# Causal mask of transposed attention scores: added by VectorE in PSUM instead of by TensorE, and score pairs taken one by one

## The chip, the cores and the metric

The kernel runs on one core of one Trainium2 chip. The metric is the device time of one execution in microseconds (us). Times of before are the median of three executions. All rows shown come from one further, profiled execution.

## What is computed

A block of a model: a linear-attention layer, a feed-forward layer, a causal softmax attention with two query sets, and the feed-forward layer again, over 2 batches of 1024 rows of 512. The change lies in the causal attention:

```
q = concatenate([q1, q2], axis=1)            # 16 heads of 32 for each set
scores = einsum('bhqd,bhkd->bhqk', q, k2) / sqrt(d)
scores = where(tril(ones((T, T))), scores, finfo.min)
p = softmax(scores, axis=-1)
y = einsum('bhqk,bhkd->bhqd', p, v2)
y1, y2 = y[:, :H], y[:, H:]
y = y1 - sigmoid(x @ Wlam) * y2
return y @ Wo
```

## The kernel before

The attention is a loop over 16 units. A unit is one batch, a group of four heads (HPT) and one of the two query sets. Its order on every engine is written out by hand, and engines meet only at semaphores.

A unit has 12 steps. Step s stands for a block of 512 queries (c = 0 in steps 0 to 3, c = 1 in steps 4 to 11) and a tile of 128 keys, kt. Scores are computed transposed, keys on the partitions and queries along the row. A step is diagonal when its key tile lies inside its query block: steps 0 to 3 and 8 to 11, eight of twelve, 128 of 192 in all. In a diagonal step the query columns before the tile are left out, so the width falls 512, 384, 256, 128.

For a step TensorE issues, in this order:

- `scores` (L1259): four score matmuls in fp32, one for each head with 32 rows of the array (L1265); four matmuls that add minus the row maximum (L1271); in a diagonal step four matmuls of an identity with `later_key`, a 128x128 matrix with -3e38 where the key lies behind the query (L1278). The first pair of heads is released to ScalarE by the second such matmul, the other pair by the fourth.
- `weigh` (L1283) of the step before: probabilities times values, four matmuls, each behind a wait for the exponential of its pair (L1295).
- `row` (L1228) for the next unit, two steps ahead: the scores once more, not transposed, four matmuls (L1237), with their own mask (L1243) in eight of the twelve. VectorE reduces them to row maxima (L1582).
- parts of jobs that fill the time (projections for the next heads L1151, values L1189, sums of the exponentials L1197, the transposed maxima L1201), and in some steps a pair of output matmuls (L1255), which VectorE adds to `x` (L1639).

ScalarE takes the exponentials of a step in two instructions, a pair of heads each (L1441), and copies jobs out of PSUM. GpSimd adds the exponentials up (L1519). VectorE does, within a step, at step 10 the negated maxima (L1592), then the two reductions of the row, the splitting of the transposed maxima into bf16 parts (step 10: L1603, L1605, L1603, L1605, L1610), the output add, and two reciprocals after steps 3, 4, 6 and 7 (L1629).

PSUM has eight banks. Six form a ring of three pairs. `PAIR_USES` lists who takes a pair and when: score pair 0, score pair 1, row pair 0, row pair 1 in each step, and an output pair in some. `take_pair` (L1215) waits until the use three places earlier has been read:

```python
kind, u, s, a = PAIR_USES[n - 3]
if kind == "row":
    pe.wait_ge(row_max, (u * NR + s) * 2 + a + 1)
elif kind == "out":
    pe.wait_ge(out_added, OUTS.index((u, s)) + 1)
else:
    pe.wait_ge(exped, (u * NS + s) * 2 + a + 1)
```

Both `scores` and `row` take their two pairs ahead of the first of four matmuls.

Of the kernel before, what the change touches and what calls it, by code (L numbers as in the profile page):

```python
# [9 lines left out]
ALU = mybir.AluOpType  # L10
# [4 lines left out]
P = 128  # L15
# [5 lines left out]
TPB = BLK // P  # L21
# [825 lines left out]
QT = S // P  # L847
HPT = P // HD
# [5 lines left out]
STEPS = [(c, kt) for c in range(CQ) for kt in range(TPB * (c + 1))]  # L854
NS = len(STEPS)
# [10 lines left out]
def step_width(s):  # L866
    c, kt = STEPS[s]
    return max(kt * P - c * BLK, 0)
# [63 lines left out]
def row_in(u, i):  # L932

    n = u * NS + i + LEAD
    return divmod(n, NR) if n < UNITS * NR else None
# [20 lines left out]
def summed_by(u, s):  # L956

    return sum(1 for t in range(NS) if STEPS[t][1]) * u + sum(1 for t in range(s + 1) if STEPS[t][1])
# [18 lines left out]
def phase_rest(nc, core, wq1, wq2, wk, wv, wlam, wo, out):  # L977
    with ExitStack() as ctx:
        sem = lambda n: ctx.enter_context(nc.semaphore("b_" + n))
# [29 lines left out]
        ident_b, later_key, mask = sb("ident_b", P, BF16), sb("later_key", P, BF16), sb("mask", P)  # L1009
# [11 lines left out]
        scored, exped, weighed, summed = sem("scored"), sem("exped"), sem("weighed"), sem("summed")  # L1021
        y_copied, y_ready, inverted, taken = sem("y_copied"), sem("y_ready"), sem("inverted"), sem("taken")
        out_done, out_added = sem("out_done"), sem("out_added")
        turn_ready, high_kept = sem("turn_ready"), sem("high_kept")
        early_var, early_root = sem("early_var"), sem("early_root")
        e_stats, e_mv = sb("e_stats", CQ * TPB * 6), sb("e_mv", CQ * TPB * 2)
# [28 lines left out]
        def strip(tile, j, lo, hi):  # L1055
            return tile[j * HD:(j + 1) * HD, lo:hi]
# [4 lines left out]
        def pair_banks(use):  # L1061
            at = PAIR_NTH[use] % 3 * 2
            return core["psum"][:, at * BLK:(at + 2) * BLK].rearrange("p (j q) -> p j q", j=2)

        def held(u, s):

            c, kt = STEPS[s]
            if kt == 0:
                return heads(total[(u * CQ + c) % 2])
            return heads(prob[(summed_by(u, s) - 1) % 2])  # L1070
# [68 lines left out]
        def _(pe):  # L1139
# [75 lines left out]
            def take_pair(use):  # L1215

                n = PAIR_NTH[use]
                if n >= 3:
# [7 lines that stand above are left out]
                return pair_banks(use)  # L1226

            def row(u, n):  # L1228
                qt, kc = ROWS[n]
                r, w = divmod(u, 2)  # L1230
                if n == 0:
                    pe.wait_ge(fill_copied, FREED_BY_ACT[NTH[("q", r, w, CQ - 1)]])
                hi = min((kc + 1) * BLK, (qt + 1) * P)
                width, diagonal = hi - kc * BLK, kc == qt // TPB
                to = [take_pair(("row", u, n, a)) for a in range(2)]
                for j in range(HPT):
                    last = pe.matmul(to[j // 2][:, j % 2, 0:width], strip(qT[w][r % 2], j, qt * P, (qt + 1) * P),  # L1237
                                     strip(kT[w][r % 2], j, kc * BLK, hi), start=True, stop=not diagonal)
                    if j % 2 and not diagonal:
                        last.then_inc(row_done, 1)  # L1240
                if diagonal:
                    for j in range(HPT):
                        last = pe.matmul(to[j // 2][:, j % 2, width - P:width], later_key[:, :], ident_b[:, :],  # L1243
                                         start=False, stop=True)
                        if j % 2:
                            last.then_inc(row_done, 1)
# [12 lines left out]
            def scores(u, s):  # L1259
                c, kt = STEPS[s]  # L1260
                r, w = divmod(u, 2)
                off, diagonal = step_width(s), kt >= TPB * c
                to = [take_pair(("score", u, s, a)) for a in range(2)]
                for j in range(HPT):
                    pe.matmul(to[j // 2][:, j % 2, off:BLK], strip(kT[w][r % 2], j, kt * P, (kt + 1) * P),  # L1265
                              strip(qT[w][r % 2], j, c * BLK + off, (c + 1) * BLK), start=True, stop=False)
                if kt == 0:
                    pe.wait_ge(bias_ready, u * CQ + c + 1)
                for j in range(HPT):
                    rows = slice(j * HD, (j + 1) * HD)  # L1270
                    last = pe.matmul(to[j // 2][:, j % 2, off:BLK], ones_b[rows, :],  # L1271
                                     bias[u % 2][rows, c * BLK + off:(c + 1) * BLK],
                                     start=False, stop=not diagonal)
                    if j % 2 and not diagonal:
                        last.then_inc(scored, 1)
                if diagonal:
                    for j in range(HPT):
                        last = pe.matmul(to[j // 2][:, j % 2, off:off + P], ident_b[:, :], later_key[:, :],  # L1278
                                         start=False, stop=True)
                        if j % 2:  # L1280
                            last.then_inc(scored, 1)

            def weigh(u, s):  # L1283
                c, kt = STEPS[s]
# [95 lines left out]
        def _(act):  # L1380
# [48 lines left out]
            def exps(u, s):  # L1429
                c, kt = STEPS[s]  # L1430
                off, g = step_width(s), u * NS + s
                if kt == 0:
                    if u:
                        act.wait_ge(filled, NTH[("den", u - 1, c)] + 1)
                elif summed_by(u, s) > 2:

                    act.wait_ge(summed, summed_by(u, s) - 2)
                    act.wait_ge(weighed, g - 1)
                for a in range(2):
                    act.wait_ge(scored, 2 * g + a + 1)  # L1440
                    act.activation(held(u, s)[:, 2 * a:2 * a + 2, off:BLK], pair_banks(("score", u, s, a))[:, :, off:BLK],  # L1441
                                   ACT.Exp, scale=SCALE).then_inc(exped, 1)

# [112 lines left out]
        def _(dve):  # L1556
# [20 lines left out]
            def row(u, n):  # L1577
                qt, kc = ROWS[n]
                width = min(BLK, (qt + 1) * P - kc * BLK)
                for a in range(2):  # L1580
                    dve.wait_ge(row_done, (u * NR + n) * 2 + a + 1)
                    dve.tensor_reduce(  # L1582
                        maxima[u % 2][:, :].rearrange("p (h q c) -> p h q c", h=HPT, q=QT)[:, 2 * a:2 * a + 2, qt, kc],
                        pair_banks(("row", u, n, a))[:, :, 0:width], AX.X, ALU.max).then_inc(row_max, 1)

            def negate(u):
                dve.wait_ge(row_max, (u + 1) * 2 * NR)
                if u:
                    dve.wait_ge(filled, NTH[("neg", u - 1)] + 1)
                part_of = neg2[:, :].rearrange("p (h n q) -> p n h q", h=HPT, n=4)  # L1590
                for n in range(3):
                    v.did(dve.tensor_reduce(part_of[:, n], maxima[u % 2][:, :].rearrange(  # L1592
                        "p (h q c) -> p h q c", h=HPT, q=QT), AX.X, ALU.max, negate=True))
                v.settle()
                dve.sem_inc(neg_ready, 1)
# [96 lines left out]
                row(*divmod(n, NR))  # L1692
            for u in range(UNITS):
                for i in range(NS):
                    if u == UNITS - 2 and (i + 1, 0) in NORM_AT:
                        early_turn(0, NORM_AT[i + 1, 0])
                    if i == NS - 2 and u + 1 < UNITS:
                        negate(u + 1)
                    if row_in(u, i):
                        row(*row_in(u, i))  # L1700
                    for place in range(2):
                        if (u, i, place) in ENDING and ON_DVE[NTH[ENDING[u, i, place]]]:
                            finish(ENDING[u, i, place])
                    if out_in(u, i):
                        add_out(*out_in(u, i))
                    if i in INVERT_AT:
                        c, half = INVERT_AT[i]
                        if u >= c:
                            invert(u - c, c, half)
                    if u == UNITS - 3 and i < QT // 2:  # L1710
                        early_stats(i)
# [118 lines left out]
```

## Time and profile before

| | |
|---|---|
| median of 3 runs | 2175.33 us (2172.42 to 2177.26) |
| profiled execution, its own time | 2175.0 us |
| its span, first to last instruction | 2172.1 us |
| TensorE busy | 2029.3 us, 93% |
| VectorE busy | 1269.5 us, 58% |
| ScalarE busy | 855.2 us, 39% |
| GpSimd busy | 888.1 us, 41% |
| attention | from about 781 us to 1800 us of the span |

PE is TensorE, PEld its weight loads, DVE VectorE, ACT ScalarE, POOL GpSimd. An fp32 matmul leaves two records, so four heads leave eight. Matmuls overlap: the row of a group gives the time from the first start to the last end, and the next group starts a little before that. A wait is shown in brackets behind the instruction that waited, with the engine and line that ended it.

### The profile page before, as it was taken

What the parts mean: (1) busy time and instruction counts of PE and PEld (TensorE: products, weight loads), DVE (VectorE), ACT (ScalarE), POOL (GpSimd) and SP (SyncE); (2) the same over time, 40 slices, a digit from 0 to 9 for tenths busy, and PEclk for the clock granted to TensorE, in tenths of its full rate; (3) what the DMA queues carried; (4) which work ended last, traced back from release to release, by engine and by line L of the source; (5) the groups of instructions that cost most, each with busy time, mean ns of one, the idle gap of its engine ahead of it and who ended that gap; (6) DMA issues with size and microseconds to landing.
All of it is one profiled execution on the core that took longest, in us unless ns stands there. A gap on an engine that the chain in (4) does not pass through costs nothing.

```text
span 2172.1 us, 29720 instructions
## 1 busy us (share of the span) xinstructions
PE 2029.3 (93%) x11783; PEld 881.1 (41%) x11824; DVE 1269.5 (58%) x1838; ACT 855.2 (39%) x1304; POOL 888.1 (41%) x457
## 2 busy tenths in 40 slices
PE   7999999999999998999999999999998878989999
PEld 3444444444444443343433333333433323444444
DVE  5878778557764643555555555555556633676635
ACT  4534344244444223333343434344343442443431
POOL 3757586400000002676665565766656682000000
PEclk9999999999999998999999999999999998999999
DMA  7101001300000030000000010000000021000001
GB/s 228 38 29 35 29 31 37 133 1 1 1 1 1 1 71 1 4 13 16 16 11 20 11 21 1 16 16 16 1 11 6 13 76 40 1 1 20 20 1 39
DMA packets 69000, 55.55 MB, mean 26 GB/s; under 512 B 36800, under 2 KB 55232, under 8 KB 68608
## 3 DMA queue, kind: packets, MB, share of 16 engines
q1 hardware_dynamic: 61952, 41.07, 6.5%
q10 hardware_dynamic: 6912, 12.59, 1.8%
q8 instruction: 95, 1.56, 0.3%
q14 instruction: 41, 0.34, 0.0%
HBM read 43.02 MB, written 10.62 MB: 25 GB/s over the span
## 4 chain that ended last, share of the span: by engine, by line
PE 50%; ACT 5%; DVE 5%; POOL 3%; issue 2%; ACTq 0%; DVEq 0%; POOLq 0%
PE psum L116 9%; PE psum L1151 8%; PE psum L1237 8%; PE psum L1265 7%; PE psum L140 5%; PE psum L1295 3%; ACT b_probs L1441 3%; PE psum L1189 3%; DVE b_maxima L1582 2%; POOL b_totals L1519 2%; PE psum L1243 2%; PE psum L1278 2%; PE psum L1255 2%; PE psum L1271 1%; PE psum L1197 1%
## 5 line engine op out<-in xcount | busy, mean ns | idle before, releaser
L1519 POOL TENSOR_TENSOR b_totals<-b_totals,b_probs 128x2048 f32<-128x2048 f32 (+3 forms) x160 | 515.2, 3220 | 350.0 <-ACT b_probs L1441 340.5
L1582 DVE TENSOR_REDUCE b_maxima<-psum 128x2 f32<-128x1024 f32 (+3 forms) x384 | 349.9, 954 | 433.1 <-PE psum L1243 249.5
L1441 ACT ACTIVATE b_probs<-psum 128x1024 f32<-128x1024 f32 (+3 forms) x320 | 228.3, 765 | 284.5 <-PE psum L1278 187.6
L435 PE MATMUL psum<-hT,a_win 128*128 128x512 f32 x640 | 290.8, 597 | 2.6 <-DVE a_parts L727 1.2
L116 PE MATMUL psum<-hT,b_early 128*128 128x512 f16 x1024 | 229.0, 383 | 5.2 <-DVE b_middle L202 5.2
L116 PE MATMUL psum<-hT,W 128*128 128x512 f16 x1024 | 229.3, 384 | 3.9 <-DVE a_win L202 3.9
L435 PEld LDWEIGHTS psum<-hT,a_win 128*128 128x128 f32 x640 | 119.4, 191 | 129.3 <-issue 128.0
L116 PEld LDWEIGHTS psum<-hT,b_early 128*128 128x128 bf16 x1024 | 100.7, 99 | 132.5 <-issue 12.1
L116 PEld LDWEIGHTS psum<-hT,W 128*128 128x128 bf16 x1024 | 101.1, 99 | 127.9 <-issue 9.4
L1496 POOL MEMSET b_mask<- 128x128 f32 x1 | 0.2, 205 | 358.8 <-POOLq L267 358.8
L1629 DVE RECIPROCAL b_down<-b_down 128x128 f32<-128x128 f32 x128 | 111.9, 917 | 43.7 <-ACT b_down L1419 43.7
L654 POOL TENSOR_TENSOR a_parts<-a_parts 128x512 bf16<-128x512 bf16 x48 | 60.1, 1252 | 132.8 <-DVE a_parts L730 132.8
L1265 PE MATMUL psum<-b_middle 32*128 32x512 f32 (+3 forms) x768 | 90.9, 542 | 22.7 <-DVE b_maxima L1582 13.2
L1237 PE MATMUL psum<-b_early 32*128 32x512 f32 (+3 forms) x768 | 90.2, 537 | 21.8 <-ACT b_probs L1441 15.1
L1441 ACT ACTIVATE b_totals<-psum 128x1024 f32<-128x1024 f32 x64 | 62.0, 1021 | 123.3 <-PE psum L1278 64.8
L1237 PE MATMUL psum<-b_middle 32*128 32x512 f32 (+3 forms) x768 | 89.1, 530 | 16.9 <-ACT b_probs L1441 14.6
L1265 PE MATMUL psum<-b_early 32*128 32x512 f32 (+3 forms) x768 | 89.4, 534 | 15.3 <-DVE b_maxima L1582 14.4
L202 DVE SCALAR_TENSOR_TENSOR a_win<-psum,a_win 128x512 f32<-128x512 f32 x64 | 44.1, 691 | 101.3 <-ACT a_win L156 100.3
L202 DVE SCALAR_TENSOR_TENSOR b_middle<-psum,lent 128x512 f32<-128x512 f32 x64 | 44.2, 691 | 96.1 <-ACT lent L156 95.5
L1151 PE MATMUL psum<-hT,b_middle 128*128 128x512 f32 x192 | 99.1, 625 | 0.0
L140 PE MATMUL psum<-W,a_yo 128*128 128x512 bf16 x256 | 97.0, 379 | 0.6
L140 PE MATMUL psum<-b_down,b_probs 128*128 128x512 bf16 x256 | 97.0, 379 | 0.6
(225 smaller groups left out, 3181.9 us busy)
## 6 DMA issues: line engine op xcount, KB each, us to landing
a_parts<-in_w_guT ACTq DMA_DIRECT2D x32, 256.0 KB, 2.8
ternary<-W SPq DMA_DIRECT2D x1, 6144.0 KB, 18.3
a_win<-in_w_inT SPq DMA_DIRECT2D x20, 256.0 KB, 7.3
a_parts<-in_w_pT ACTq DMA_DIRECT2D x16, 256.0 KB, 2.6
b_down<-lam_rows SPq DMA_DIRECT2D x32, 128.0 KB, 2.7
b_early<-ternary SPq DMA_DIRECT2D x8, 512.0 KB, 8.3
out<-x SPq DMA_DIRECT2D x16, 256.0 KB, 2.2
x<-in_x SPq DMA_DIRECT2D x3, 1024.0 KB, 8.0
```

The costliest lines, as they stand in the source:

```text
L116: last = pe.matmul(self.bank[m % 2 * 2 + part], self.gu[:, k * 2 * HID + col:k * 2 * HID + col + P], self.hT[:, at:at + BLK], start=(k + h ...
L140: last = pe.matmul(self.down_bank(j, t), src[:, m * BLK + t * P:m * BLK + (t + 1) * P], self.wd[:, m * D:(m + 1) * D], start=(m + half == ...
L202: dve.scalar_tensor_tensor(self.h[:, m * BLK:(m + 1) * BLK], self.bank[m % 2 * 2 + 1], 1.0 / UP, self.sg[m % 2], ALU.mult, ALU.mult).then_ ...
L435: last = pe.matmul(ring(s, j), win[:, at:at + P], core["hT"][:, (i * KT + k) * BLK:(i * KT + k + 1) * BLK], start=(k == 0), stop=(k == KT ...
L1151: return pe.matmul(to, weights[:, k * P:(k + 1) * P], hT[:, at:at + BLK], start=(k == 0), stop=(k == KT - 1))
L1189: last = pe.matmul(to[:, t % 2 * 2 * P:(t % 2 + 1) * 2 * P], hT[:, at:at + P], wv_all[:, k * D + h * P:k * D + (h + 2) * P], start=(k == 0 ...
L1237: last = pe.matmul(to[j // 2][:, j % 2, 0:width], strip(qT[w][r % 2], j, qt * P, (qt + 1) * P), strip(kT[w][r % 2], j, kc * BLK, hi), star ...
L1265: pe.matmul(to[j // 2][:, j % 2, off:BLK], strip(kT[w][r % 2], j, kt * P, (kt + 1) * P), strip(qT[w][r % 2], j, c * BLK + off, (c + 1) * B ...
L1441: act.activation(held(u, s)[:, 2 * a:2 * a + 2, off:BLK], pair_banks(("score", u, s, a))[:, :, off:BLK], ACT.Exp, scale=SCALE).then_inc(ex ...
L1519: pool.tensor_tensor(acc, acc, held(u, s)[:, :, off:BLK], ALU.add).then_inc(summed, 1)
L1582: dve.tensor_reduce(maxima[u % 2][:, :].rearrange("p (h q c) -> p h q c", h=HPT, q=QT)[:, 2 * a:2 * a + 2, qt, kc], pair_banks(("row", u, ...
L1629: last = dve.reciprocal(rden[k % 2][:, cols], rden[k % 2][:, cols])
```

## The change

`scores` no longer issues the third group of four matmuls in diagonal steps. The second matmul of each pair of heads in L1271 releases it. VectorE gets `cap`, which waits for a pair and adds `mask` (fp32, the same -3e38 pattern) to the 128 diagonal columns of both heads, in place in PSUM. ScalarE waits in diagonal steps for `capped` instead of `scored`. `cap` of a step stands first in VectorE's work of that step. In `scores` and in `row` the second pair is taken behind the first pair's two matmuls.

```diff
-                to = [take_pair(("row", u, n, a)) for a in range(2)]
+                to = []
                 for j in range(HPT):
+                    if j % 2 == 0:
+                        to.append(take_pair(("row", u, n, j // 2)))
...
-                off, diagonal = step_width(s), kt >= TPB * c
-                to = [take_pair(("score", u, s, a)) for a in range(2)]
+                off = step_width(s)
+                to = []
                 for j in range(HPT):
+                    if j % 2 == 0:
+                        to.append(take_pair(("score", u, s, j // 2)))
...
-                                     start=False, stop=not diagonal)
-                    if j % 2 and not diagonal:
+                                     start=False, stop=True)
+                    if j % 2:
                         last.then_inc(scored, 1)
-                if diagonal:
-                    for j in range(HPT):
-                        last = pe.matmul(to[j // 2][:, j % 2, off:off + P], ident_b[:, :], later_key[:, :],
-                                         start=False, stop=True)
-                        if j % 2:
-                            last.then_inc(scored, 1)
...
                 for a in range(2):
-                    act.wait_ge(scored, 2 * g + a + 1)
+                    if kt >= TPB * c:
+                        act.wait_ge(capped, (u * QT + kt) * 2 + a + 1)
+                    else:
+                        act.wait_ge(scored, 2 * g + a + 1)
...
+            def cap(u, s):
+                c, kt = STEPS[s]
+                off = step_width(s)
+                if kt >= TPB * c:
+                    for a in range(2):
+                        dve.wait_ge(scored, 2 * (u * NS + s) + a + 1)
+                        own = pair_banks(("score", u, s, a))[:, :, off:off + P]
+                        dve.tensor_tensor(own, own, mask[:, :].unsqueeze(1).to_broadcast([P, 2, P]),
+                                          ALU.add).then_inc(capped, 1)
...
                 for i in range(NS):
+                    cap(u, i)
                     if u == UNITS - 2 and (i + 1, 0) in NORM_AT:
```

## Rows read from the trace of the kernel before

**Rows 1.** Busy time by engine over unit 7, with counts, granted clock and DMA.

```profile
1268.00:1329.00 61.00, 58.80 (x477) 24.44 (x478) 33.09 (x43) 22.72 (x32) 39.44 (x17) 1.00 0.09 18
```

**Rows 2.** Waits in the attention: total us, times, longest us.

```profile
PE psum L1237 <- ACT b_probs L1441: 29.7, 68, 1.3
PE psum L1265 <- DVE b_maxima L1582: 27.6, 48, 1.4
```

**Rows 3.** Timeline of unit 7, steps 7 and 8: start us, us, engine, line.

```profile
1303.51 0.39 PE L1271 MATMUL psum<-b_last_bias,b_ones_b 32*128 32x512 bf16 x4
1303.83 1.06 PE L1295 MATMUL psum<-b_probs,b_middle 128*32 128x512 f32 x8
...
1304.01 1.94 ACT L1441 ACTIVATE b_probs<-psum 128x1024 f32<-128x1024 f32 x2 [3.69 <-PE psum L1271]
...
1308.10 1.75 DVE L1629 RECIPROCAL b_down<-b_down 128x128 f32<-128x128 f32 x2
...
1309.11 0.39 PE L1271 MATMUL psum<-b_last_bias,b_ones_b 32*128 32x512 bf16 x4
...
1309.76 1.06 PE L1295 MATMUL psum<-b_probs,b_middle 128*32 128x512 f32 x8
1309.84 1.94 ACT L1441 ACTIVATE b_probs<-psum 128x1024 f32<-128x1024 f32 x2 [0.99 <-PE psum L1278]
...
1311.01 1.14 PE L1237 MATMUL psum<-b_early 32*128 32x512 f32 x8 [0.18 <-ACT b_probs L1441]
```

**Rows 4.** Groups of the attention by form: busy us, mean ns of one.

```profile
L1441 ACT ACTIVATE b_probs<-psum 128x512 f32<-128x512 f32 x64 | 34.7, 595 | 35.3 <-PE psum L1278 31.7 <-POOL b_totals L1519 3.4
...
L1582 DVE TENSOR_REDUCE b_maxima<-psum 128x2 f32<-128x256 f32 x58 | 21.9, 421 | 35.4 <-PE psum L1243 35.4
...
L1605 DVE SCALAR_TENSOR_TENSOR psum<-b_rounded,b_after_part,psum 128x128 f32<-128x128 bf16 x30 | 10.7, 356 | 1.1
```

**Rows 5.** Timeline of unit 7, steps 2 and 3.

```profile
1279.21 0.29 PE L1271 MATMUL psum<-b_last_bias,b_ones_b 32*128 32x256 bf16 x4
...
1279.84 1.09 ACT L1441 ACTIVATE b_probs<-psum 128x512 f32<-128x512 f32 x2 [0.46 <-PE psum L1278]
1280.58 1.14 PE L1237 MATMUL psum<-b_early 32*128 32x512 f32 x8
...
1283.11 0.50 PE L1265 MATMUL psum<-b_middle 32*128 32x128 f32 x8 [0.40 <-DVE b_maxima L1582]
```

**Rows 6.** Timeline of unit 6 (even), steps 10 and 11.

```profile
1260.58 1.22 DVE L1639 TENSOR_TENSOR x<-x,psum 128x1024 f32<-128x1024 f32 x1 [1.31 <-PE psum L1255]
1260.94 0.29 PE L1271 MATMUL psum<-b_middle,b_ones_b 32*128 32x256 bf16 x4
...
1262.31 0.50 PE L1237 MATMUL psum<-b_early 32*128 32x128 f32 x8
...
1263.93 0.26 PE L1271 MATMUL psum<-b_middle,b_ones_b 32*128 32x128 bf16 x4
...
1265.06 0.71 PE L1237 MATMUL psum<-b_early 32*128 32x256 f32 x8
1265.16 0.29 DVE L1610 CAST b_negT<-psum 128x128 bf16<-128x128 f32 x1
```

**Rows 7.** Timeline of unit 7 (odd), step 11.

```profile
1324.40 0.23 PE L1271 MATMUL psum<-b_last_bias,b_ones_b 32*128 32x128 bf16 x4
...
1324.58 1.21 DVE L1639 TENSOR_TENSOR x<-x,psum 128x1024 f32<-128x1024 f32 x1
...
1325.84 0.71 PE L1237 MATMUL psum<-b_early 32*128 32x256 f32 x8 [0.31 <-DVE x L1639]
```

**Rows 8.** Timeline of unit 6, step 2: its row matmuls.

```profile
1219.08 1.14 PE L1237 MATMUL psum<-b_middle 32*128 32x512 f32 x8 [1.34 <-ACT b_probs L1441]
```

**Rows 9.** Engines by stretch: after unit 0's stalls, and the like of unit 6.

```profile
849.00:856.00 7.00, 5.61 (x43) 2.87 (x40) 3.12 (x4) 0.66 (x2) 3.08 (x2) 0.55 0.01 2
1218.00:1225.00 7.00, 5.52 (x55) 2.45 (x56) 3.56 (x5) 2.65 (x6) 3.61 (x2) 1.00 0.00 0
```

More of the change, by code:

```diff
@@ L1023, in phase_rest @@
         out_done, out_added = sem("out_done"), sem("out_added")
+        capped = sem("capped")
         turn_ready, high_kept = sem("turn_ready"), sem("high_kept")
```

## The prediction

> **What bounds the kernel now.** I read the page first: TensorE is busy for 93% of the span, no other engine for more than 58%. The four edits all lie in the attention part, 16 units of 12 steps, so I took one unit by engine [rows 1]: in 61 us TensorE is busy for 58.80, VectorE for 33.09, ScalarE for 22.72, GpSimd for 39.44. TensorE has 2 us of rest per unit, so in the attention what is taken from its queue is time, and so is every stall put into it. The waits of the attention [rows 2] say where the rest goes: TensorE stands before the row matmuls L1237 for the exponentials (29.7 us, 68 times) and before the score matmuls L1265 for the row maxima (27.6 us, 48 times). Both come from the ring of three pairs of banks. A step takes four places in it: score pair a=0, a=1, row pair a=0, a=1. Row pair 1 therefore gets the banks of score pair 0 of the same step, and can't start before `exped` of that pair.
>
> The timeline of two steps shows that loop closed [rows 3]. Step 7 has no mask: biases L1271 at 1303.51, weigh L1295 at 1303.83, first exponential at 1304.01, 0.50 after the biases. Step 8 has masks: biases 1309.11, weigh 1309.76, first exponential 1309.84, 0.73 after the biases. It lasts 1.02 (half of a pair of 1.94, which overlap) and ends at 1310.86; the row matmuls start at 1311.01, 0.15 later, after 0.18 of idle time. So in step 8 the chain scores, mask, exponential, row matmul sets the pace, and TensorE only waits. In step 2 [rows 5] the exponential starts 0.63 after the biases, lasts 0.60 [rows 4], and with the 0.15 ends at 1.38; the row matmuls start at 1.37 (1280.58 less 1279.21). The chain and TensorE's own queue arrive together: slack nil. I read steps 1, 3, 9, 10 and 11 of the same unit in the same way, rows of the same pattern: slack nil but for an add in the odd units' step 11 (below). Step 0 alone, with a fill ahead of its rows, has 0.19.
>
> **Removed: 512 mask matmuls.** Biases to weigh is 0.65 with them and 0.32 without [rows 3]: 0.33 us of TensorE for each of 128 diagonal steps, 42 us in all. It is time only where TensorE's own queue decides when the row matmuls start. Where the chain decides, what counts is the way to the first exponential.
>
> **Added: 256 VectorE adds, on that chain.** Without the masks the first exponential would start 0.50 after the biases instead of 0.73. The add goes between. Its cost isn't in the trace: a reduction that reads as many elements (128x256) from PSUM takes 0.42, and the one group that writes PSUM from VectorE, L1605, takes 0.36 for half as many [rows 4]. From that 0.42 to the 1.22 of L1639, with 1024 elements from PSUM [rows 6], is 1.04 ns an element, so L1605's form at 256 would be 0.49. I take 0.49, as the add writes PSUM too; 0.42 is the lower bound, and 0.60 the upper one, if a hand-over between two more engines costs another 0.1. Starting VectorE and then ScalarE costs little beyond what the 0.50 holds already; I give it 0.01. The first exponential starts 1.00 after the biases: 0.27 later than before at full width, and by the same count 0.25, 0.27 and 0.24 in the narrower steps. The second add (over before the first exponential is) hides behind ScalarE. The Trainium skill, "VectorE: DVE Perf Modes", errata table, has 120 cycles plus one per element at 0.96 GHz for a PSUM source, an estimate of 0.39 us here; the rows above are longer (0.42 for the same size), and by the page's figure the sum below would be about 10 us smaller.
>
> **VectorE must also be free.** It works in order, and `cap` of a step stands behind what the step before left it. In step 8 the two reciprocals L1629 run from 1308.10 to 1309.85, 0.74 past the biases [rows 3], where the add could start at 0.41; instructions that don't wait start about 0.08 before their forerunner ends, so the add starts at 0.67: 0.26 more. In step 10 of an even unit the output add L1639 lasts to 1261.80, 0.86 past the biases [rows 6]: 0.48 more; in an odd unit nothing is in the way there. Step 11 is the worst: the five instructions that split the row maxima end with L1610 at 1265.45, 1.52 past the biases [rows 6], where the add could start at 0.25: 1.19 more. In odd units L1639 comes after the split and ends at 1325.79, 1.39 past the biases; the row matmuls waited for it already, to 1.44 [rows 7]. The add then starts at 1.30, the exponential (0.38 long) at 1.89, and row pair 1 at 2.42: 0.98 later than now.
>
> **Moved: pairs one by one.** The score matmuls gain nothing, since the biases follow all four. Row pair 0 may start while pair 1 waits. It ends the step no sooner: eight records of four heads run together in 1.14 [rows 3], and pair 1 needs the same from its own start. It helps in one place. The row of step 2 has no mask of its own, so its first reduction starts with pair 0; the scores of step 3 stand 0.40 for that reduction [rows 5], and this 0.40 goes. In even units step 2 itself stands 1.34 for an exponential that ScalarE's four copies hold up [rows 8]; there neither masks nor adds matter, 0. For odd units VectorE's second reduction still stands in front of step 3's add, 0.15.
>
> **The sum**, per unit, steps 0, 1, 2, 3, 8, 9, 10, 11:
> even: 0.08 + 0.25 + 0 + (0.24 - 0.40) + (0.27 + 0.26) + 0.27 + (0.27 + 0.48) + (0.24 + 1.19) = 3.15 us;
> odd: 0.08 + 0.25 + 0.28 + (0.24 + 0.15 - 0.40) + (0.27 + 0.26) + 0.27 + 0.27 + 0.98 = 2.66 us.
> Steps 4 to 7 are unchanged: no mask, and their chain stays. Six even and seven odd units (1 to 13) give 37.5. Unit 0 I put at 1, because its step 3 now stands 1.4 us for the same reduction. In units 14 and 15 rows run out and GpSimd's adds set the pace: 1.5 for both. Together 40 us. The profiled execution took 2175.0 (span 2172.1 and 2.9 around it), the median is 2175.3: 2215.
>
> **Rivals.**
> The masks' time is kept (on the other side). The chain takes the add in its stride, and 42 us go: 2133. This decides at one number: the add and its hand-over must cost less than the 0.23 that the way to the exponential shortens (0.73 to 0.50). Nothing on VectorE that touches 256 elements of PSUM is near it, and steps 8, 10 and 11 have VectorE occupied in any case. A milder form: exponentials late by a few tenths, given back by pair 0's head start. That needs row pairs that don't share the array well; the 1.14 for eight records of 512 columns speaks against it. 9 in 100 for faster, 5 for a sum near nil.
>
> The clock falls. In unit 0, after stalls of 1.34 and 1.40 within some 4 us, the granted clock was 0.55 over the 7 us that follow, 43 matmul records instead of 55 in the like stretch of unit 6 [rows 9]: 1.5 us lost per fall. Step 11 will stall for about 1.3 in even units, with 0.38 shortly before. If that does it each time, and in some odd units too, 8 to 15 falls cost 12 to 22 us: 2228 to 2238, with doubled stalls behind them at most 2250. Against it: the single stall of 1.34 in the other even units left it at 1.00 [rows 9]. The Trainium skill, "TensorE: Matmul & The Clock Gate", Part 1, says that idle time takes the array from 2.4 to 1.2 GHz; by that rule more waits could only bring more falls, none fewer. 12 in 100.
>
> The split breaks up the four heads. Were a group of four, cut by a wait, to run as two groups each of nearly its full time, every step would lose up to 2 x 0.8 us: 192 steps, up to 300 us, about 2450. Against it: weigh has a wait before each head, and its eight records still take 1.06 together [rows 3]. 4 in 100.
>
> VectorE as the bound: 16 adds of 0.49 are 8 us on 33 of 61 per unit [rows 1]; no.
>
> **How the numbers follow.** My forecast has 70 in 100, the clock 12, the broken group 4, faster 9, nil 5. Each gated step pays the add in full, some seven in a unit: the lower bound of 0.42 takes 7 us from the sum, the upper of 0.60 adds 11; if VectorE is late by half of what I read, 12 go. The likeliest case alone spans 2204 to 2227. The range to 2240 takes in the clock. Within 0.2% (4.4 us, about what a measurement of this kernel tells from no change) I count 5 in 100, faster 8, slower 87.
>
> **What would show it.** L1278 gone and weigh 0.32 after the biases in every step. The new add at 0.42 to 0.50, its first one of step 11 starting 1.4 after the biases. The first exponential of masked steps 1.0 after the biases. The wait of L1237 for exponentials grown from 30 us to some 110, in steps 8, 10 and 11 above all, and the wait of L1265 in step 3 gone. TensorE's busy time about 40 lower with a longer span, VectorE's 110 to 125 higher. I am wrong if the row matmuls of steps 10 and 11 start as early as now: then the add isn't behind what I put it behind, or the exponential doesn't gate them.

## The result: slower by 1.0%, less than forecast

| | median | lowest to highest |
|---|---|---|
| before | 2172.42 us | 2168.71 to 2177.26 |
| changed | 2194.92 us | 2191.11 to 2196.9 |

The ratio is 1.0099, with a 95% interval of 1.0079 to 1.0119: 17 to 26 us more. The forecast was 2215 us, 2204 to 2240. The direction was right; the size was twice too large, and the measured time lies below the range.

The profile after has a span of 2191.6 us, 19.5 above that of before. First the page (the engines' busy times, and the group of the new adds) and, below the dots, five rows of its waits in us, times, longest, and one of the kernel with masks alone (second experiment):

```profile
PE 2086.6 (95%) x11312; PEld 904.4 (41%) x11312; DVE 1362.4 (62%) x2094; ACT 855.6 (39%) x1304; POOL 888.5 (41%) x457
...
L1595 DVE TENSOR_TENSOR psum<-psum,b_mask 128x256 f32<-128x256 f32 x256 | 97.1, 425 | 58.5 <-PE psum L1276 58.4
```

```profile
ACT b_probs L1443 <- DVE psum L1595: 215.2, 96, 4.7
...
PEld psum L1240 <- ACT b_probs L1443: 61.0, 97, 2.0
...
PE psum L1240 <- ACT b_probs L1443: 22.0, 42, 1.2
...
PEld psum L1270 <- DVE b_maxima L1584: 15.1, 20, 1.0
...
PE psum L1270 <- DVE b_maxima L1584: 1.3, 3, 0.6
```

```profile
PE psum L1238 <- ACT b_probs L1439: 112.4, 145, 2.2
```

The add takes 0.425 us, and the second one of a pair starts 0.32 to 0.34 behind the first, so VectorE's busy time grows by 93 us, not by 110 to 125. ScalarE now waits for VectorE. The waits of the row matmuls for exponentials stand in two rows, 61.0 us on the weight loads and 22.0 on the matmuls. They can't be added, as one stall shows in both (in step 11 below as 1.46 and 1.05), and the matmuls' row leaves out what passes while row pair 0 is still counted as running. With the pairs taken jointly the row is comparable to that of before: it grows from 29.7 [rows 2] to 112.4 with masks alone, where some 110 were forecast. The score matmuls' wait for the row maxima is 1.3 instead of 27.6; their weight loads wait 15.1. TensorE's busy time is 57 us higher, although 512 matmuls are gone: a row group that is cut in two is counted as busy twice, 1.13 for each half, where four heads together counted 1.14 [rows 3]. That figure says nothing of work here.

Steps 7 and 8 of unit 7 in the timeline after (start us, us, engine, line), the same place as [rows 3]:

```profile
1315.18 0.39 PE L1276 MATMUL psum<-b_last_bias,b_ones_b 32*128 32x512 bf16 x4
...
1315.50 1.06 PE L1294 MATMUL psum<-b_probs,b_middle 128*32 128x512 f32 x8
1315.68 1.94 ACT L1443 ACTIVATE b_probs<-psum 128x1024 f32<-128x1024 f32 x2 [3.58 <-PE psum L1276]
...
1319.66 1.75 DVE L1641 RECIPROCAL b_down<-b_down 128x128 f32<-128x128 f32 x2
...
1320.67 0.39 PE L1276 MATMUL psum<-b_last_bias,b_ones_b 32*128 32x512 bf16 x4
...
1321.00 1.06 PE L1294 MATMUL psum<-b_probs,b_middle 128*32 128x512 f32 x8
1321.33 0.74 DVE L1595 TENSOR_TENSOR psum<-psum,b_mask 128x256 f32<-128x256 f32 x2
1321.86 1.94 ACT L1443 ACTIVATE b_probs<-psum 128x1024 f32<-128x1024 f32 x2 [1.44 <-DVE psum L1595]
1321.99 0.30 PEld L1240 LDWEIGHTS psum<-b_early 32*128 32x128 f32 x4 [0.84 <-issue]
1321.99 1.13 PE L1240 MATMUL psum<-b_early 32*128 32x512 f32 x4
...
1322.93 0.30 PEld L1240 LDWEIGHTS psum<-b_early 32*128 32x128 f32 x4 [0.64 <-ACT b_probs L1443]
```

In the masked step 8 weigh follows the biases by 0.33, as without a mask. The add starts 0.66 behind the biases, held by the reciprocals (0.67 was forecast). The first exponential starts 1.19 behind them (0.73 before) and ends at 1322.88. Row pair 0 has started long before, at 1321.99. Pair 1 starts at 1322.93, which is **0.05 behind the exponential's end, not the 0.15 of [rows 3]**.

Steps 10 and 11 of unit 6, the place of [rows 6]:

```profile
1270.90 1.22 DVE L1651 TENSOR_TENSOR x<-x,psum 128x1024 f32<-128x1024 f32 x1 [1.31 <-PE psum L1258]
...
1271.26 0.29 PE L1276 MATMUL psum<-b_middle,b_ones_b 32*128 32x256 bf16 x4
...
1272.04 0.76 DVE L1595 TENSOR_TENSOR psum<-psum,b_mask 128x256 f32<-128x256 f32 x2
...
1273.23 0.49 PE L1240 MATMUL psum<-b_early 32*128 32x128 f32 x4 [0.47 <-ACT b_probs L1443]
...
1274.78 0.22 PE L1276 MATMUL psum<-b_middle,b_ones_b 32*128 32x128 bf16 x2
...
1276.08 0.29 DVE L1622 CAST b_negT<-psum 128x128 bf16<-128x128 f32 x1
1276.28 0.75 DVE L1595 TENSOR_TENSOR psum<-psum,b_mask 128x256 f32<-128x256 f32 x2
...
1276.82 0.66 ACT L1443 ACTIVATE b_probs<-psum 128x256 f32<-128x256 f32 x2 [3.15 <-DVE psum L1595]
1277.26 0.30 PEld L1240 LDWEIGHTS psum<-b_early 32*128 32x128 f32 x4 [1.46 <-ACT b_probs L1443]
1277.26 0.70 PE L1240 MATMUL psum<-b_early 32*128 32x256 f32 x4 [1.05 <-ACT b_probs L1443]
```

Here the forecast holds: the add of step 11 stands behind the last of the five splitting instructions, 1.50 behind the second pair's biases, and row pair 1 stands 1.05 for its exponential, in every even unit from 0 to 12.

I measured each step from its first score matmul to that of the next, in every kernel, and took the difference to the kernel before (us, two decimals). Units without a change of the clock repeat to 0.01 in all steps but 10 and 11, which vary by up to 0.07:

```
step                  0    1    2    3    4    5    6    7    8    9   10   11    sum
even, forecast      .08  .25    0 -.16    0    0    0    0  .53  .27  .75 1.43   3.15
even, after        -.24  .13 -.57  .14 -.42  .32 -.11 -.10  .36  .13  .14 1.72   1.49
odd,  forecast      .08  .25  .28 -.01    0    0    0    0  .53  .27  .27  .98   2.66
odd,  after        -.24  .13 -.34  .42 -.42  .04 -.10 -.11  .35  .13  .13  .84   0.82
```

Steps 1 and 6 to 9 are 0.10 to 0.18 below the forecast, and of these 6 and 7 have no mask, so that the change of masks does not touch them. In steps 0, 2 to 5, 10 and 11 the start of the score matmuls itself has moved, which shifts time between neighbours; taken together they are below the forecast as well. So the split of the pairs, forecast to help at one place, helps everywhere.

### The profile page after: what moved, and what is told of

The parts are those of the page before. It is cut to its first block, busy times and chain, and to the rows that moved or that the text cites. A ratio compares the mean times of both kernels' runs of the same rounds, so it can differ in the third digit from the quotient of the medians.

```text
span 2191.6 us, 28626 instructions
## 1 busy us (share of the span) xinstructions
PE 2086.6 (95%) x11312; PEld 904.4 (41%) x11312; DVE 1362.4 (62%) x2094; ACT 855.6 (39%) x1304; POOL 888.5 (41%) x457
## 4 chain that ended last, share of the span: by engine, by line
PE 51%; DVE 6%; ACT 4%; POOL 3%; issue 2%; ACTq 0%; DVEq 0%; POOLq 0%
PE psum L1240 10%; PE psum L116 9%; PE psum L1152 8%; PE psum L1270 6%; PE psum L140 5%; PE psum L1294 5%; PE psum L1190 3%; POOL b_totals L1521 2%; DVE b_maxima L1584 2%; PE psum L1246 2%; PE psum L1258 2%; ACT b_probs L1443 1%; PE psum L1276 1%; PE psum L1198 1%; DVE psum L1595 1%
## 5 line engine op out<-in xcount | busy, mean ns | idle before, releaser
L1240 PE MATMUL psum<-b_middle 32*128 32x512 f32 (+3 forms) x768 | 135.7, 537 | 16.3 <-ACT b_probs L1443 13.0
L1240 PE MATMUL psum<-b_early 32*128 32x512 f32 (+3 forms) x768 | 131.0, 539 | 14.5 <-ACT b_probs L1443 9.1
L1595 DVE TENSOR_TENSOR psum<-psum,b_mask 128x256 f32<-128x256 f32 x256 | 97.1, 425 | 58.5 <-PE psum L1276 58.4
L1270 PE MATMUL psum<-b_middle 32*128 32x512 f32 (+3 forms) x768 | 105.7, 541 | 5.9 <-ACT b_probs L1443 4.6
L1270 PE MATMUL psum<-b_early 32*128 32x512 f32 (+3 forms) x768 | 98.3, 538 | 0.7 <-DVE b_maxima L1584 0.7
L1240 PEld LDWEIGHTS psum<-b_middle 32*128 32x128 f32 x768 | 53.4, 184 | 107.8 <-issue 62.8
```

The lines of the kernel that those rows point to most:

```text
L1595: dve.tensor_tensor(own, own, mask[:, :].unsqueeze(1).to_broadcast([P, 2, P]), ALU.add).then_inc(capped, 1)
```

## The experiments

Each ratio is to the kernel before on the same chip, with its 95% interval. Time differences per unit and step are read as in the table above.

**Split alone.** Masks stay on TensorE; only the pairs are taken one by one.

```diff
-                to = [take_pair(("row", u, n, a)) for a in range(2)]
+                to = []
                 for j in range(HPT):
+                    if j % 2 == 0:
+                        to.append(take_pair(("row", u, n, j // 2)))
...  (and the same in scores)
```

> Both masks stay on TensorE; scores and row matmuls take their pairs one by one. Theory A (the add costs some 40 to 50 us on the chain to the exponential, and taking pairs one by one gives more than 20 back): 20 to 28 us faster than the kernel before, about 2148, with the waits before the score matmuls for row maxima nearly gone and row pair 1 starting 0.05 us after its exponential instead of 0.14. Theory B (the split does next to nothing and the add costs only some 22): within 3 us of the kernel before.

Measured: 2151.06 us (2149.16 to 2152.44), ratio 0.9901 (0.9876 to 0.9925), 1.39 less in an even and 1.08 less in an odd unit. The split is worth 21 us, not the 0.40 in one step of the prediction.

**Masks alone.** VectorE adds them; both pairs are taken ahead of the first matmul, as before.

```diff
-                to = []
+                to = [take_pair(("row", u, n, a)) for a in range(2)]
                 for j in range(HPT):
-                    if j % 2 == 0:
-                        to.append(take_pair(("row", u, n, j // 2)))
...  (and the same in scores)
```

> The mask is added by VectorE; both pairs are taken ahead of the first matmul, as before. Theory A: 45 to 55 us slower than the kernel before (2217 to 2227), so slower than the whole change by 25 or so; by my step sums redone with the add at its measured place, 3.6 us per even and 2.9 per odd unit, and some falls of the clock. Theory B: 20 to 25 us slower, like the whole change.

Measured: 2245.46 (2240.68 to 2246.34), ratio 1.0331 (1.0304 to 1.0358); 3.52 more in an even, 2.92 in an odd unit. Without the gain of its split the forecast would have been 3.55 and 3.06. The price of the masks alone came out right, in even units by luck: the adds and what holds them cost 0.33 less than forecast over the other masked steps, and step 3 costs 0.30 more, because VectorE's second reduction holds its add there too. The sum as a whole erred in what the split gives. That makes 42 us of the 73 in units 1 to 13. In the profiled execution the clock falls 15 times between the first step of the attention and its last, where before has 4; in units 0 to 12 it is 9 times against once. In units 1 to 12 the time above that of the fastest units comes to 16 us.

**No mask of the transposed scores.** Neither engine masks them, so later keys count in the exponentials; pairs as before.

```diff
-                                         start=False, stop=True)      # mask matmuls L1278 left out
-            ... cap left out, ScalarE waits for scored
```

> Leaves the mask of the transposed scores out altogether, so probabilities of later keys stay in; pairs are taken jointly. It prices the removed half of the change by itself. If the way to the first exponential gates row pair 1, a diagonal step gains what that way shortens, 0.23 us, some 27 to 33 us in all (about 2142). If TensorE's own queue decided, it would gain 0.33 a step, 42 us (2130). If the masks were hidden, nothing.

Measured: 2147.63 (2147.52 to 2149.85), ratio 0.9889 (0.986 to 0.9918). Six of the eight masked steps give 0.23 to 0.24 us, which is 0.73 less 0.50, the shortened way to the exponential, and not the 0.33 of TensorE's work. Step 0 gives 0.33, as TensorE's own queue is behind there; step 2 of even units and step 11 of odd ones give nothing. So with joint pairs the chain sets the pace in the masked steps but for these, as [rows 3] was read.

**One more reduction of 128x256 ahead of each add** (whole change otherwise), to see whether VectorE's time is on the path:

```diff
+                        dve.tensor_reduce(spent[:, m % 4 * 2:m % 4 * 2 + 2], own, AX.X, ALU.max)
                         dve.tensor_tensor(own, own, wide, ALU.add).then_inc(capped, 1)
```

> The whole change, with one more VectorE instruction, a reduction of the same 256 elements, ahead of each add (its result is not used). Theory A (VectorE's work before the exponential is on the chain in seven of eight masked steps of a unit): 0.34 to 0.42 us later in about 100 steps, 35 to 45 us slower than the whole change, 2230 to 2240. Theory B (the adds are mostly covered and the loss comes from somewhere else, such as the clock): under 15 us slower.

Measured: 2241.21 (2238.39 to 2242.47), ratio 1.0314 (1.0288 to 1.034): 46 us more than the change. An odd unit has 2.32 more over its eight masked steps, 0.33 in six of them, which is the start-to-start time of two such instructions (0.29 in step 8, 0.05 in step 3). VectorE's time ahead of the exponential is paid in full. The attention has 13 falls of the clock, the changed kernel 5, so that part of the 46 us is the clock's.

**Which half of the split?** First the rows joint again, then the scores joint again, on top of the whole change.

```diff
@@ row, in the first @@
-                    if j % 2 == 0:
-                        to.append(take_pair(("row", u, n, j // 2)))
+                to = [take_pair(("row", u, n, a)) for a in range(2)]
@@ scores, in the second @@
-                    if j % 2 == 0:
-                        to.append(take_pair(("score", u, s, j // 2)))
+                to = [take_pair(("score", u, s, a)) for a in range(2)]
```

> The whole change, but the row matmuls take both pairs ahead of the first, as before; only the scores take them one by one. Theory A (most of what the split gives comes from the rows: row pair 1, its wait standing in the middle of running matmuls, starts about 0.09 us sooner after the exponential in some ten steps of a unit, and row pair 0 runs ahead): 20 us or more slower than the whole change, 2215 to 2225. Theory C (it comes from the scores, whose first pair no longer waits for the row maximum that only the second pair needs): at most 10 slower.

> The whole change, but the scores take both pairs ahead of the first matmul; only the rows take them one by one. Theory A: 5 to 15 us slower than the whole change. Theory C: 20 or more slower, near the 2245 of the run with both taken jointly.

Measured: rows joint 2242.26 (2238.83 to 2242.84), ratio 1.0325 (1.0299 to 1.035), no better than masks alone. Scores joint 2194.13 (2191.18 to 2201.5), ratio 1.0111 (1.008 to 1.0142), as good as the whole change. The rows' half carries the gain. With it step after step is 0.105 shorter, and steps 2 and 3 together are 0.98 shorter in even and 0.70 in odd units.

**The add of step 11 ahead of the splitting** of the row maxima, in even units:

```diff
-                    cap(u, i)
+                    if i < NS - 1 or u % 2:
+                        cap(u, i)
...
+                        if i == NS - 2 and place == 0 and u % 2 == 0:
+                            cap(u, NS - 1)
```

> The whole change, but in even units VectorE does the add of step 11 ahead of the splitting of the row maxima, not behind it. Theory A (in step 11 of even units the add waits for the split, 1.7 us, and the stall lets the granted clock fall in some units): 1.4 us less in each of 8 even units and no falls right after them, 12 to 20 us faster than the whole change, 2175 to 2183. If only the clock mattered and the stall had cover: 8. If the split is itself urgent (GpSimd makes the next unit's bias from it), the wait moves to the biases of step 0 and nothing is gained.

Measured: 2177.78 (2174.97 to 2180.97), ratio 1.0034 (1.0022 to 1.0045). The timeline of unit 6, step 11:

```profile
1261.18 0.22 PE L1276 MATMUL psum<-b_middle,b_ones_b 32*128 32x128 bf16 x2
...
1261.41 0.77 DVE L1595 TENSOR_TENSOR psum<-psum,b_mask 128x256 f32<-128x256 f32 x2 [0.28 <-PE psum L1276]
...
1262.39 0.19 PEld L1240 LDWEIGHTS psum<-b_early 32*128 32x128 f32 x2 [0.20 <-ACT b_probs L1443]
```

The add starts 0.23 behind the second pair's biases instead of 1.50, and the weight load of row pair 1 waits 0.20 instead of 1.46; its matmuls, which stood 1.05, now start while pair 0's are still running. The medians are 17 us apart, the ratios, each to before on its own chip, 14. Step 11 costs 0.46 instead of 1.72, in all 9 us over the even units 0 to 12. Most of the rest is the clock's: in units 0 to 12 it falls once, at 1325, behind a step 11 of an odd unit, where the changed kernel has four falls.

**No mask, and pairs one by one** (later keys count here too):

> Leaves the mask of the transposed scores out, so probabilities of later keys stay in, and takes the pairs one by one. It tells what the mask costs once the split is there. If TensorE's own queue then decides, 0.33 us for each of some 120 steps: 35 to 40 us faster than the split alone, about 2113. If the way to the exponential still gates, 0.23 a step: 25 to 28, about 2124.

Measured: 2121.57 (2116.71 to 2122.11), ratio 0.9766 (0.9736 to 0.9796). That is 29.5 us below the split alone, between the two expectations, and bounds what another way of masking could still gain in this order of work. Step by step against the split alone, six masked steps give 0.28 to 0.33, step 8 gives 0.23, and one gives nothing (step 2 in even units, step 11 in odd ones). So once the pairs are taken one by one and no mask is in the way, TensorE's own queue decides in most masked steps.

**Only the order of two waits.** Masks alone, as in the second experiment, with the waits of the two row pairs in the other order; matmuls and their order unchanged.

```diff
-                to = [take_pair(("row", u, n, a)) for a in range(2)]
+                to = [take_pair(("row", u, n, a)) for a in (1, 0)][::-1]
```

> Masks by VectorE and both pairs taken jointly, as in the second experiment, but the row matmuls' two waits stand in the other order: the one for row pair 1 (for the exponential) first, so that another of the two conditions is waited for by an instruction of its own. Theory A (the split gains because in the joint form the exponential's wait stands on a separate instruction ahead of the weight load, which puts the first row matmul 0.144 us behind the exponential's end instead of 0.05): with the exponential's wait on the weight load itself, the gap falls to about 0.05, and with some 11 gated steps in each of 16 units the time falls by 10 to 20 us, to 2225 to 2235. Theory B (it gains because row pair 0 is ahead by then, whatever carries the wait): the gap may shrink or not, the time stays at the 2245 of the second experiment, within 5 us. If the gap stays at 0.144, the swap has not reached what it was to change, and A stands untested.

Measured: 2230.25 (2223.89 to 2234.11), ratio 1.0266 (1.0239 to 1.0292), some 14 us less (the two ratios differ by 0.0065) with no head start for anyone. Unit 2, step 8, first masks alone, then with the waits swapped:

```profile
1008.35 1.94 ACT L1439 ACTIVATE b_probs<-psum 128x1024 f32<-128x1024 f32 x2 [1.45 <-DVE psum L1591]
1009.49 0.29 PEld L1238 LDWEIGHTS psum<-b_middle 32*128 32x128 f32 x5 [1.85 <-issue]
1009.52 0.71 PE L1238 MATMUL psum<-b_middle 32*128 32x512 f32 x4 [0.97 <-ACT b_probs L1439]
```

```profile
1008.10 1.94 ACT L1439 ACTIVATE b_probs<-psum 128x1024 f32<-128x1024 f32 x2 [1.45 <-DVE psum L1591]
1009.18 0.20 PEld L1238 LDWEIGHTS psum<-b_middle 32*128 32x128 f32 x4 [1.79 <-ACT b_probs L1439]
1009.18 0.71 PE L1238 MATMUL psum<-b_middle 32*128 32x512 f32 x4 [0.88 <-ACT b_probs L1439]
```

One exponential lasts 1.02, so the first ends at 1009.37 in the one and at 1009.12 in the other. The row matmuls start 0.15 and 0.06 behind it. The single instructions of the trace say why. First `take_pair`'s wait for `exped` as the view of its line has it (duration in ns, first and last start), in masks alone between 1009.0 and 1009.6 and in the whole kernel before; then the first row matmul with the waits swapped:

```profile
L1226 PEldq EVENT_SEMAPHORE  x1: 51/51/51, 1009.4 to 1009.4; - x1
```

```profile
L1225 PEldq EVENT_SEMAPHORE  x191: 51/51/51, 836.9 to 1792.5; - x191
```

```profile
L1238 PEld LDWEIGHTS psum<-b_middle x1: 181/181/181, 1009.2 to 1009.2; 32*128 32x128 f32 x1
```

In the joint form the wait for `exped` is an instruction of its own (EVENT_SEMAPHORE, 0.051 long, at 1009.411), the weight load with the other, long satisfied wait follows at 1009.486 and the matmul at 1009.517. Swapped, the weight load itself carries the wait for `exped` and starts at 1009.177, with its matmul at 1009.179. The Trainium skill, "Perfetto Trace Analysis", Identifying Dependency Chains, says that an instruction that waits on several engines may get EventSemaphore instructions ahead of it for the further conditions. The trace agrees. What such an instruction costs the page doesn't say; here it is 0.09. In both orders the wait that the program issued first stayed on the weight load, and the one behind it became the separate instruction. The changed kernel has no such instruction from `take_pair`, the kernel before 191 of this one.

**Where the split must be, with masks on TensorE.** The rows alone one by one, and the first experiment's kernel beside it:

> Masks by TensorE as before; of the splits that of the row pairs alone, the score pairs taken jointly. The gain of the split lies in the rows: 2152, within 3 us of the first experiment (2151). Rival: the score matmuls' own split counts as well once the masks are back on TensorE; then 4 to 8 us more than the first experiment, 2155 to 2159.

> The first experiment's kernel once more, on the chip of the two beside it, so that they can be compared: 2151, ratio to the kernel before 0.990.

Measured: rows alone 2156.36 (2152.99 to 2159.85), ratio 0.9928 (0.9907 to 0.9948); both 2150.11 (2149.42 to 2152.26), ratio 0.9898 (0.9872 to 0.9924). The rival was right: with masks on TensorE the scores' split counts too, 6 us, although it was worth nothing in the total on top of VectorE's masks. Its gain per unit is there in both cases (0.18 even, 0.47 odd after; 0.20 and 0.49 here); with VectorE's masks the profiled execution has two more falls of the clock in units 0 to 12 than the one with the scores joint, and in units 1 to 12 they cost some 5 us more, where the scores' half gives 4.4 in units 1 to 13. Where the scores are taken jointly, TensorE stands 0.35 ahead of step 5's for a row maximum, and the total of such waits in the score matmuls' row is 17.2 us against 1.3 with them one by one. No run tells these places apart.

**The order of the waits in the kernel before**, nothing else:

> The kernel before, with nothing changed but the order of the row matmuls' two waits (the one for row pair 1, on the exponential, stands first). Theory: the wait instruction of its own ahead of the weight load costs the 0.09 us in every step in which the exponential comes last, with or without the change. Those are steps 0, 2 and 5 to 9 at least in each unit (and 1, 3, 10, 11 by less, where TensorE's own queue arrives with the chain, 0.04 there), some 0.6 to 0.9 per unit: 10 to 14 us less, 2158 to 2163. Rival: where TensorE's own queue and the chain arrive together, the earlier start only moves the wait to the next take; then 2170 to 2173, no difference.

Measured: 2164.81 (2160.84 to 2166.37), ratio 0.9958 (0.9943 to 0.9973), 8 us less, a little under what was expected. Steps 5 to 8 gain 0.09 each. Steps 1, 3, 9 and 10 gain 0.03 to 0.04, step 2 0.08 in even units and 0.03 in odd ones, and step 0 nothing: there TensorE's queue arrives just behind the chain. In odd units step 11 gives 0.09 back.

## Why the sign was right and the size wrong

**What was right.** The chain scores, mask, exponential, row matmul sets the pace of masked steps (no mask: 0.23 back, not 0.33; one more VectorE instruction: paid in full). The masks' 42 us on TensorE were no gain, so the rival in which they are kept fell. VectorE's occupied moments were read rightly in steps 8 (0.66 against 0.67), 10 and 11. With the masks alone the units cost 3.52 and 2.92 against 3.55 and 3.06, with two errors that cancel in the even ones (second experiment). In step 3 it erred: joint, the add is held 0.34 by the second reduction, in both kinds of unit; with the split only odd units keep that, 0.29 instead of the 0.15 of the sum.

**The step that failed** is "Moved: pairs one by one": a gain of 0.40 in step 3 and nothing else ("It helps in one place"), with "The score matmuls gain nothing" and the hand-over of 0.15 kept in every step. The split gave 2.03 us in an even and 2.10 in an odd unit. The differences to the kernel before, in us per unit, as the edits come in:

```
                                      even   odd
masks alone                           3.52   2.92
+ waits swapped                       2.57   1.97    0.09 in each of some ten steps
+ rows one by one (scores joint)      1.67   1.29    0.90 and 0.68, of them 0.80 and 0.53 in steps 2 and 3
+ scores one by one (the change)      1.49   0.82
```

Half or more of the rows' gain has nothing to do with pair 0's head start, and the sum held that to be the whole effect. I took the 0.15 from the exponential's end to the row matmul as the time of the hand-over itself, and so kept it in the new chain. It held 0.09 of a separate wait instruction, which the split removes, as each pair's wait then rides on its own weight load. That is 0.105 in eleven gated steps with the head start, 0.09 without. The place that I did name, step 3, gives 0.47 where 0.40 was forecast, and in even units the 0.34 more by which VectorE is free for the add, which the sum had counted. "The score matmuls gain nothing" was wrong by 0.18 in even and 0.47 in odd units. That "pair 1 needs the same from its own start" held: four staggered heads free the next work 1.06 after pair 1 starts, as joint ones do.

**The balance.** Units 1 to 13 without falls of the clock come to 6 x 1.49 + 7 x 0.82 = 14.7 instead of 37.5. Of these 22.8 us less, 15.0 are the 0.105 in eleven steps of 13 units, 4.4 the scores' half, for which the prediction had 0, 0.9 the 0.07 more of step 3, and the remaining 2.5 mostly the add's smaller size (the exponential of step 0 starts 0.95 behind the biases, not 1.00), less the 0.15 by which odd units' step 3 is held longer. Unit 0 came to -2.7 instead of 1: with step 3's stall the fall of [rows 9] went too. Units 14 and 15 came to -4.4 instead of 1.5. Falls in units 1 to 12 added 9.1, unit 13 stands 1.1 above the other odd ones, the stretch behind the last step's start is 1.1 longer, and the one ahead of the first step 0.4. 40 - 22.8 - 3.7 - 5.9 + 9.1 + 1.1 + 1.1 + 0.4 = 19.3, with 19.5 in the spans. For units 13 to 15 and the stretches around the attention's steps these are readings; their causes were not tried.

**The clock** was a rival, and part of it came true. Engines by stretch, around the stall of unit 2's step 11 and where [rows 9] has unit 0's fall:

```profile
1020.00:1027.00 7.00, 6.37 (x20) 2.69 (x24) 2.75 (x5) 0.66 (x2) 3.07 (x3) 0.52 0.01 2
```

```profile
849.00:856.00 7.00, 6.17 (x59) 2.86 (x54) 2.65 (x5) 1.28 (x3) 3.31 (x2) 1.00 0.01 2
```

In unit 2 TensorE stood 0.41 and then, four microseconds later, 1.05, and over 1020 to 1027 the granted clock was 0.52, near 1.2 GHz. The clock fell at step 11 of units 0, 2, 4 and 12, which cost 1.6 to 3.0 us each. In units 6, 8 and 10 the same stall of 1.05 left it at 1.00. The shorter stall ahead of it doesn't separate them: 0.41 in unit 2 and 0.47 in units 4 and 12, but also 0.47 in units 6 and 8 and 0.41 in unit 10, and none over 0.15 in unit 0. Unit 0's old fall is gone (0.55 before, 1.00 now). With the add moved ahead of the splitting that stall was gone and none of these four was left; one came elsewhere, behind a stall of 0.84. The Trainium skill, "TensorE: Matmul & The Clock Gate", Part 1, has idle time take the array from 2.4 to 1.2 GHz; in these runs falls went with stalls, but equal stalls of 1.05 were followed by one or not, and what decides between them is not shown. In the kernels with longer stalls (masks alone, rows joint, one more reduction, waits swapped) there were 13 to 16 falls in the attention, 8 to 10 of them in units 0 to 12: the mechanism of the rival, at the price it had, but only with stalls that the split took away again.

The split of four heads into two groups broke nothing, and VectorE at 62% is no bound.

## What to carry to other kernels

Before you keep a hand-over time from a trace in a sum, look at the single instructions in it. Where an instruction waits for two things, issue first the wait that comes true last, so that it stays on the instruction itself: a take of several buffers ahead of one matmul puts a wait instruction between, 0.09 us each time here, and swapping two waits alone gave 8 us. Split such takes. And leave the mask on TensorE, which hands the scores to ScalarE in any case, instead of putting VectorE between the two: the kernel with the split alone, 2150 to 2151 us, is faster than both. When work moves to an in-order engine, cost what stands ahead of it there; moving one add ahead of five instructions gave 14 to 17 us.

## What was unexpected of the hardware

- The instruction that only waits takes 0.051 us, the weight load follows 0.075 behind its start, and its matmul another 0.031; with the wait on the weight load the matmul follows the load by 0.002. From the exponential's end to the matmul it is 0.147 against 0.05.
- An in-place add of 128x256 in PSUM takes 0.425, hardly more than a reduction of as many elements (0.421), and a second starts 0.32 to 0.34 behind the first. The 0.49 that was put together from L1605's form [rows 4] was too much for a second operand from SBUF.
- Of seven equal stalls of 1.05 us four went with a fall of the clock and three did not.
